# Column tile by column tile in three matmul stages, and PSUM evictions of the low-rank FFN moved from ScalarE to VectorE

## What is computed

```python
x = x + 0.5 * ffn(layernorm(x))
x = x + attn(layernorm(x))
x = x + 0.5 * ffn(layernorm(x))
def ffn(x):                       # ranks 1024 -> 256 -> 4096 -> 256 -> 1024
    P = x @ U1
    H = gelu(P @ V1 + b1)
    Q = H @ U2
    return Q @ V2 + b2
def attn(x):
    h, gate = split(x @ in_proj_w.T)          # 2048 each
    h = (causal_conv4(h, groups=8) + conv_b) * silu(gate)
    m = silu(layernorm(h) @ fc_w.T + fc_b) @ cproj_w.T + cproj_b
    return (m + h) @ out_w.T
```

## Time and profile before

| | us |
|---|---|
| median of 3 runs | 1602.27 (1602.11 to 1605.39) |
| profiled execution | 1608.78 |
| its span on the slowest core (5) | 1607.7 |
| spans of the 8 cores | 1594.6 to 1607.7 |
| TensorE matmul busy | 1158.5 (72%) |
| VectorE busy | 484.2 (30%) |
| ScalarE busy | 428.1 (27%) |
| mean granted TensorE clock, core 5 | 0.885 |

### The profile page before, as it was taken

The page is one execution under the profiler, slowest core; times in us unless marked ns, Lnnn a source line. Parts: engine busy times, 40 slices in busy tenths (PEclk is TensorE's granted clock), DMA queues, the critical chain, the costliest instruction groups (busy, mean ns, idle before and its releaser), DMA issues.

```text
span 1607.7 us, 15188 instructions; the slowest of 8 cores (1594.6 to 1607.7 us)
## 1 busy us (share of the span) xinstructions
PE 1158.5 (72%) x5480; PEld 472.9 (29%) x5480; DVE 484.2 (30%) x606; ACT 428.1 (27%) x776; POOL 23.2 (1%) x47
## 2 busy tenths in 40 slices
PE   0348744999955999847754876389997399986675
PEld 0023211444421444312322322134443044432232
DVE  0162144112247033252125222421213802324311
ACT  0344431121120100124544443212122110011444
POOL 0000000000000000000000000000000000000000
PEclk9969976999985999979986899689999599998899
DMA  9700000234220333260110000023242024420011
GB/s 144 174 1 0 1 1 0 54 65 79 43 49 1 76 60 75 53 160 27 53 53 1 1 0 0 1 40 79 40 79 53 0 53 79 79 53 0 0 53 53
DMA packets 14296, 73.65 MB, mean 46 GB/s; under 512 B 2576, under 2 KB 2576, under 8 KB 8720
## 3 DMA queue, kind: packets, MB, share of 16 engines
q0 software_dynamic: 6208, 55.58, 18.7%
q1 hardware_dynamic: 8016, 17.10, 3.1%
HBM read 119.86 MB, written 8.39 MB: 80 GB/s over the span
## 4 chain that ended last, share of the span: by engine, by line
PE 61%; DVE 17%; ACT 10%; issue 6%; DMA 4%; another core or an unknown queue 1%; DVEq 0%; ACTq 0%; POOL 0%; SPq 0%; POOLq 0%
PE pb L779 8%; PE pb L516 8%; PE pb L833 7%; PE pb L810 7%; PE pb L1022 7%; PE pb L1074 7%; PE pb L987 6%; ACT h L507 5%; PE pb L498 5%; DVE varb L396 3%; DVE hn L947 3%; DMA wslot<-ip_blob 3%; DMA y<-outb 2%; DVE xcur_sb L665 1%; DVE xn L741 1%
## 5 line engine op out<-in xcount | busy, mean ns | idle before, releaser
L507 ACT ACTIVATE h<-pb,consts_sb 128x512 bf16<-128x512 f32 (+1 forms) x320 | 165.2, 620 | 116.0 <-PE pb L498 115.8
L516 PE MATMUL pb<-h,ffn_sb 128*128 128x512 bf16 (+1 forms) x640 | 122.0, 344 | 58.3 <-ACT h L507 58.3
L987 PE MATMUL pb<-hn,wslot 128*128 128x512 bf16 x512 | 133.7, 416 | 38.6 <-DVE hn L947 37.9
L779 PE MATMUL pb<-xn,wslot 128*128 128x512 bf16 (+1 forms) x768 | 135.4, 324 | 34.5 <-DVE xn L749 34.5
L498 PE MATMUL pb<-h,ffn_sb 128*128 128x512 bf16 (+1 forms) x640 | 138.4, 350 | 20.9 <-ACT h L477 10.2
L850 DVE SCALAR_TENSOR_TENSOR h<-pb,consts_sb,gate 128x512 bf16<-128x512 f32 x64 | 48.0, 751 | 294.1 <-PE pb L833 294.0
L833 PE MATMUL pb<-ph,wslot 128*128 128x512 bf16 x512 | 116.0, 379 | 0.0
L810 PE MATMUL pb<-xn,wslot 128*128 128x512 bf16 x512 | 115.7, 379 | 0.0
L1074 PE MATMUL pb<-h,wslot 128*128 128x512 bf16 x512 | 113.3, 379 | 3.4 <-DVE h L1037 3.4
L791 ACT CAST ph<-pb 128x512 bf16<-128x512 f32 (+1 forms) x96 | 43.6, 454 | 262.6 <-PE pb L779 262.5
L1022 PE MATMUL pb<-m,wslot 128*128 128x512 bf16 x512 | 110.8, 379 | 2.6 <-ACT m L1001 2.6
(11 more groups left out here) (89 smaller groups left out, 946.1 us busy)
## 6 DMA issues: line engine op xcount, KB each, us to landing
wslot<-ip_blob POOLq DMA_DIRECT2D x16, 1536.0 KB, 12.4
wslot<-fc_blob POOLq DMA_DIRECT2D x8, 1024.0 KB, 8.1
wslot<-cp_blob POOLq DMA_DIRECT2D x8, 1024.0 KB, 8.1
wslot<-ow_blob POOLq DMA_DIRECT2D x8, 1024.0 KB, 8.2
y<-outb SPq DMA_DIRECT2D x32, 256.0 KB, 2.1
ffn_sb<-ffn_blob POOLq DMA_DIRECT2D x1, 5120.0 KB, 36.8
xcur_sb<-x SPq DMA_DIRECT2D x1, 4224.0 KB, 23.2
xcur_sb<-x SPq DMA_DIRECT2D x2, 2048.0 KB, 63.4
```

The source lines that it names most:

```text
L507: c2 = E.inc("s", s.activation(Hqb[:, mq * 512:mq * 512 + w], pt[bi][:, :w], AF.Gelu_apprx_tanh, bias=ccol("b1", m), scale=1.0))
L516: ii = t.matmul(pt[u2[mu]][:, :w], fftile("U2", k, mu), Hqb[:, kq * 512:kq * 512 + w], start=(qq == 0 and kq == 0), stop=(qq == 3 and kq = ...
L779: ii = t.matmul(pt[bi][:, :w], ws_tile(ci, "ip", ("Wh", k, ml)), xn[:, k * TH + tcol:k * TH + tcol + w], start=(k == 0), stop=(k == 7))
L987: ii = t.matmul(pt[fcb_banks[si5]][:, :w], ws_tile(ci, "fc", ("fc", m % 2, k)), hn[:, k * HT + t0o:k * HT + t0o + w], start=(k == 0), stop ...
```

## The change

- The two copies of P and the two of Q in ffn_tile go from ScalarE to VectorE (tensor_copy). There are five tiles in a half.
- In fc, cproj and out_w the column tile becomes the outer loop and k the inner one. A tile's bank is evicted behind its own matmuls, and in out_w flush3() is called between the two tiles' matmuls. In cproj the same is done as in fc.
- dst_add2: VectorE computes 0.5 * product + bias from PSUM into the outb slot (tensor_scalar) and then adds the residual to the slot in a second operation. ScalarE's multiplication and tsl are gone.

```diff
@@ -472,12 +472,12 @@
                         cnt = E.inc("t", ii)
                         E.note_w("t", bk, cnt)
                         E.note_r("t", B_xsrc, cnt)
-                        E.r_wait("s", bk)
-                        E.w_wait("s", B_Pb_c[0])
-                        c2 = E.inc("s", s.copy(Pb_c[0][:, m * 512:m * 512 + w],
-                                               pt[bi][:, :w]))
-                        E.note_r("s", bk, c2)
-                        E.note_w("s", B_Pb_c[0], c2)
+                        E.r_wait("v", bk)
+                        E.w_wait("v", B_Pb_c[0])
+                        c2 = E.inc("v", v.tensor_copy(Pb_c[0][:, m * 512:m * 512 + w],
+                                                      pt[bi][:, :w]))
+                        E.note_r("v", bk, c2)
+                        E.note_w("v", B_Pb_c[0], c2)
                     if after_u1 is not None:
                         after_u1()
                     u2a = nb(held=avoid)
@@ -523,12 +523,12 @@
                                 E.note_w("t", banks[u2[mu]], cnt)
                     for mu in range(2):
                         bk = banks[u2[mu]]
-                        E.r_wait("s", bk)
-                        E.w_wait("s", B_Qb_c[0])
-                        c2 = E.inc("s", s.copy(Qb_c[0][:, mu * 512:mu * 512 + w],
-                                               pt[u2[mu]][:, :w]))
-                        E.note_r("s", bk, c2)
-                        E.note_w("s", B_Qb_c[0], c2)
+                        E.r_wait("v", bk)
+                        E.w_wait("v", B_Qb_c[0])
+                        c2 = E.inc("v", v.tensor_copy(Qb_c[0][:, mu * 512:mu * 512 + w],
+                                                      pt[u2[mu]][:, :w]))
+                        E.note_r("v", bk, c2)
+                        E.note_w("v", B_Qb_c[0], c2)
                     for m in range(8):
                         bi = nb(held=avoid)
                         bk = banks[bi]
@@ -976,31 +976,26 @@
                                 ccol("fc_b", m, 1)))
                             E.note_r("v", bk, c2)
                             E.note_w("v", B["fcb"], c2)
-                        fcb_banks = [nb(), None]
-                        fcb_banks[1] = nb(held=(fcb_banks[0],))
-                        for bi in fcb_banks:
-                            E.w_wait("t", banks[bi])
-                        for k in range(16):
-                            E.wait("t", "vc", hn_ready[k])
-                            for si5, (tcol, w) in enumerate(OWN_TILES):
-                                t0o = tcol - HALO
-                                ii = t.matmul(pt[fcb_banks[si5]][:, :w],
+                        for (tcol, w) in OWN_TILES:
+                            t0o = tcol - HALO
+                            bi = nb()
+                            bk = banks[bi]
+                            E.w_wait("t", bk)
+                            for k in range(16):
+                                E.wait("t", "vc", hn_ready[k])
+                                ii = t.matmul(pt[bi][:, :w],
                                               ws_tile(ci, "fc", ("fc", m % 2, k)),
                                               hn[:, k * HT + t0o:k * HT + t0o + w],
                                               start=(k == 0), stop=(k == 15))
-                                if k == 15:
-                                    cnt = E.inc("t", ii)
-                                    E.note_w("t", banks[fcb_banks[si5]], cnt)
-                        E.note_r("t", B_hn, E.cnt["tc"])
-                        for si5, (tcol, w) in enumerate(OWN_TILES):
-                            t0o = tcol - HALO
-                            bk = banks[fcb_banks[si5]]
+                            cnt = E.inc("t", ii)
+                            E.note_w("t", bk, cnt)
+                            E.note_r("t", B_hn, cnt)
                             E.r_wait("s", bk)
                             E.w_wait("s", B_m1)
                             E.r_wait("s", B["fcb"])
                             c2 = E.inc("s", s.activation(
                                 m1[:, m * HT + t0o:m * HT + t0o + w],
-                                pt[fcb_banks[si5]][:, :w], AF.Silu,
+                                pt[bi][:, :w], AF.Silu,
                                 bias=fcb[:, m:m + 1], scale=1.0))
                             E.note_r("s", bk, c2)
                             E.note_w("s", B_m1, c2)
@@ -1011,31 +1006,26 @@
                         ci = half * 20 + 12 + m // 4
                         if m % 4 == 0:
                             ws_ensure(ci)
-                        cpb = [nb(), None]
-                        cpb[1] = nb(held=(cpb[0],))
-                        for bi in cpb:
-                            E.w_wait("t", banks[bi])
-                        for k in range(8):
-                            E.r_wait("t", B_m1)
-                            for si5, (tcol, w) in enumerate(OWN_TILES):
-                                t0o = tcol - HALO
-                                ii = t.matmul(pt[cpb[si5]][:, :w],
+                        for (tcol, w) in OWN_TILES:
+                            t0o = tcol - HALO
+                            bi = nb()
+                            bk = banks[bi]
+                            E.w_wait("t", bk)
+                            for k in range(8):
+                                E.r_wait("t", B_m1)
+                                ii = t.matmul(pt[bi][:, :w],
                                               ws_tile(ci, "cp", ("cp", m % 4, k)),
                                               m1[:, k * HT + t0o:k * HT + t0o + w],
                                               start=(k == 0), stop=(k == 7))
-                                if k == 7:
-                                    cnt = E.inc("t", ii)
-                                    E.note_w("t", banks[cpb[si5]], cnt)
-                        E.note_r("t", B_m1, E.cnt["tc"])
-                        for si5, (tcol, w) in enumerate(OWN_TILES):
-                            t0o = tcol - HALO
-                            bk = banks[cpb[si5]]
+                            cnt = E.inc("t", ii)
+                            E.note_w("t", bk, cnt)
+                            E.note_r("t", B_m1, cnt)
                             base = m * HT + t0o
                             E.r_wait("v", bk)
                             E.r_wait("v", B["consts"])
                             E.dep("v", B_h)
                             c2 = E.inc("v", v.scalar_tensor_tensor(
-                                h[:, base:base + w], pt[cpb[si5]][:, :w],
+                                h[:, base:base + w], pt[bi][:, :w],
                                 ccol("cproj_b", m, 1), h[:, base:base + w],
                                 ALU.add, ALU.add))
                             E.note_r("v", bk, c2)
@@ -1064,25 +1054,19 @@
                     if m % 2 == 0:
                         ws_ensure(ci)
                     for si, (tcol, w) in enumerate(OWN_TILES):
+                        t0o = tcol - HALO
                         bi = mm_banks[si][m % 2]
-                        E.w_wait("t", banks[bi])
-                    for k in range(16):
-                        E.r_wait("t", B_h)
-                        for si, (tcol, w) in enumerate(OWN_TILES):
-                            t0o = tcol - HALO
-                            bi = mm_banks[si][m % 2]
+                        bk = banks[bi]
+                        E.w_wait("t", bk)
+                        for k in range(16):
+                            E.r_wait("t", B_h)
                             ii = t.matmul(pt[bi][:, :w],
                                           ws_tile(ci, "ow", ("ow", m % 2, k)),
                                           h[:, k * HT + t0o:k * HT + t0o + w],
                                           start=(k == 0), stop=(k == 15))
-                            if k == 15:
-                                cnt = E.inc("t", ii)
-                                E.note_w("t", banks[bi], cnt)
-                    E.note_r("t", B_h, E.cnt["tc"])
-                    for si, (tcol, w) in enumerate(OWN_TILES):
-                        t0o = tcol - HALO
-                        bi = mm_banks[si][m % 2]
-                        bk = banks[bi]
+                        cnt = E.inc("t", ii)
+                        E.note_w("t", bk, cnt)
+                        E.note_r("t", B_h, cnt)
                         flush3()
                         base = m * HT + t0o
                         E.r_wait("v", bk)
@@ -1186,24 +1170,22 @@
 
                     def dst_add2(m, bi, bk, _si=si, _t0o=t0o, _tcol=tcol, _w=w):
                         sl = m % 2
-                        E.r_wait("s", bk)
-                        E.w_wait("s", B_tsl[sl])
-                        c3 = E.inc("s", s.mul(tsl[:, sl * 512:sl * 512 + _w],
-                                              pt[bi][:, :_w], 0.5))
```

(20 more changed lines are left out.)

## The result

The changed kernel took 1626.5 us (median of 8 runs), the kernel before 1605.4 on the same chip: a ratio of 1.014, 95% interval 1.0124 to 1.0156, so 21 us slower by the medians and 22 to 23 by the ratio. Forecast were +12.3 us and a range that ended at 1623. The sign was right; the size was not. (In some executions, whatever the kernel, cores of one half of the chip ran at a lower granted clock and took longer; the ratios and intervals leave these out, the medians do not.)

What follows compares the result with a forecast made beforehand. TensorE holds 61% of the chain of waits, so VectorE or ScalarE edits matter only where TensorE waits. Gains of 24.4 and losses of 36.7 make +12.3 us on 1602.3, so 1614.6 us; range 1603 to 1623.

Steps and rivals of the forecast that it cites:

- The out_w stage: In out_w, matmuls of one column tile cover the other's statistics chain: period 9.41 to 8.15 us, gain 10.5 per half.
- What VectorE pays for PSUM copies: A VectorE copy of 128x512 f32 from PSUM takes 0.69 us, 0.62 start to start; bounds 0.42 and 0.69.
- VectorE reads PSUM fast: Rival: VectorE's copies from PSUM take 0.42 us each, so the net is +1.0 us, 1603; chance 0.12.
- fc, m=0: In fc's first m, 15 matmuls formerly hidden come after hn is ready: 3.25 us lost per half, 6.5 in all.
- P copies: In FFN 1, copies queue on VectorE behind other work: per half +5.8 us in tile 2, +1.2 tile 1, +0.4 tile 0.
- The stage borders: At two stage borders one eviction remains: waits of 1.35 and 1.71 us become 0.77 and 0.85, gaining 1.44 per half.
- The output of FFN 2: Both VectorE operations hold the store slot, so output pairs come 3.85 or 3.69 us apart; loss 14.6 us together.
- the -0.25 for each tile 0: In FFN 2's tile 0 the P copy is 0.1 us slower but ScalarE's casts come sooner: -0.25 us per half.
- Tile 1 of half 1: In half 1's FFN 2, tile 1's hidden layer starts at 1558.2 against 1554.49: at most +3.7 us.
- The last tile's outputs: FFN 2's tile 1 outputs take 14.0 us against 11.0: +2.9 us in half 0, +2.3 at the kernel's end.
- the clock stays down longer: Rival: 10 more slow matmuls at each of four TensorE restarts add 8.4 us, net +20.7, 1623; chance 0.15.
- the likeliest case: The prediction's own sum of terms, net +12.3 us, with own range +7 to +18 (1609 to 1620); chance 0.68.

Runs made afterwards that it cites:

- the paired version: Loop order of fc, cproj and out_w alone, but fc's m=0 keeps both column tiles under each k; 1581.1 us, 0.985 of the kernel before.
- the best version: Loop order with fc's m=0 paired, plus four FFN 2 store slots instead of two, ScalarE still multiplying; 1565.0 us, 0.9743 of the kernel before.

## Why the prediction was right and wrong

**Right.** *The out_w stage*: period 8.16 against 8.15, gain 77.64 - 67.32 = 10.3 against 10.5. *What VectorE pays for PSUM copies*: 0.69, start to start 0.60 where I had 0.62; "VectorE reads PSUM fast" fell. *fc, m=0*: some 6 us by the paired version, 6.5 forecast, of which 5 lie in the edited stage. *P copies*: +6.3 in tile 2 against +5.8; tile 1's row product on core 3 comes 33.0 us after the reciprocal instead of 31.35, +1.65 against 1.2 + 0.4. The two FFN 1 stages together gave +15.9 against +15.2; that they agree so well is partly luck, since one by one they gave +9.7 and +6.2 for 7.6 each. *The stage borders* gave half: 1.35 became 1.21 (first row of cproj, core 3) and 1.71 became 1.07, in place of 0.77 and 0.85.

**Wrong.** The step that failed is "The output of FFN 2", whose 14.6 was mis-sized (its four terms measure 5.5 + 6.0 + 3.4 + 2.7 = 17.6), and beside it the -0.25 for each tile 0 (+0.9 and +0.7). For FFN 2 as a whole the terms make +14.5 (14.6, -0.5 and 0.4 of the Q copies); +19.3 was measured, 4.8 more. By medians over the cores, from TensorE's marks in the two stages:

- *Tile 1 of half 1*, 2.3. I priced it "from 1542.3 with 3.85" against 1554.49, "less because one store was late there already", as +3.7. That late store was the slowest core's own (its stage took 128.0 us, the median core's 125.59). From the output product of tile 0 to tile 1's hidden layer the cores lost +6.0; half 0 lost +5.5 against +5.7 forecast. That wait has two causes where I had one: the release of the banks (the output alone has +2.4 and +2.7) and the P copies behind the outputs.
- *Tile 0 of both halves*, 2.1. From the P product to the hidden layer I had -0.25 each; it was 6.11 before and 7.03 after, and 6.60 and 7.32. The copy and its hand-over are some 0.1 of that. The rest is the product itself: its 16 matmuls took 5.3 us on every core before and 5.6 or 6.5 after, in half 1 5.8 and 6.4. With no P copy moved, the output change alone shows 6.5 in half 1 on seven cores of eight, and the loop order alone 6.3 to 6.4 on six. So it is the clock's level at the restart and not the copies; that it moves with the shift in time is my reading, which no run tested by itself.
- *The last tile's outputs*, 0.9: +3.4 and +2.7 where "+2.9" and "+2.3" stood (its own figures make 3.0 and 2.2). The first operation takes 748 ns, not 690.

These are 5.3; half 0's tile 1 and the pieces between, up to 0.6 each and of both signs, give 0.5 back. Further misses: 1.0 in the normalization-to-out_w stages (mostly the borders), 0.7 in FFN 1, 0.3 in conv, 0.2 at the start. Together 7.0: +19.3 by the median core where I had +12.3. From there to the 24.2 us between 1602.3 and 1626.5, 3.1 are the baseline (three runs gave a median of 1602.3, eight 1605.4), and 1.8 are left. They are not a wider spread of the cores: in the timed runs the slowest core lies 4.6 us above the median core after the change and lay 3.9 to 6.1 above it before. They fit a profile before that was some 3 us long. So the forecast missed the median core by about 9 us, of which the stages show 7.0.

Of the rival "the clock stays down longer" a part may have come true: 192 matmuls per core at the lower level against 180, by the count described with the Q copies, 12 x 0.211 = 2.5 us where it had 8.4. But core by core the count moved by -30 to +40, so these 12 alone do not show it.

**Do the parts add up?** Not all. By the median core of the timed runs: loop order -17.0, P +22.6, output +16.2, Q +8.2, together +30.0; the whole has +21.5. The P copies are worth 22 to 23 alone and in the whole. Without them the whole has -0.6, and the other three parts add up to +7.4. The 8 us between are about what the Q copies cost alone beyond my 0.8; in the whole that cost is not there. (Sums over stages, 16.2 to 19.5 for the parts and 19.3 for the whole, seem to agree, but the output's part in them counts the cores at the lower clock.) Nor do the stages add up one by one. Half 1's fc restart costs +1.86 in the kernels with Q or output alone and nothing with P alone. Half 1's FFN 1 moves by -3.75 in the loop order with no edit of its own there; in the profile before, five cores took 148.7 to 149.4 us in it and three 144.9 to 145.5, so a part of this can be the reference's own. What I gave as the own range of the likeliest case, +7 to +18, had no allowance for such shifts of the clock, nor for a baseline of three runs; with some 3 us for each its upper end would have been about where the time fell.

## What to carry to other kernels

Moving an operation to an "idler" engine puts it behind everything that engine has queued: look first at what stands ahead of it in program order and who waits (here eight bias adds and a square; 22 to 23 us for 20 copies, four of them narrow). Where an engine writes into a store slot, count how long the slot is held and let the operation that frees a PSUM bank not wait for it; two more slots were worth 16 us. A dependent chain is best hidden behind a whole block of other matmuls, but not where the producer is the slow one: there pair up the work to use the wait.

Price a phase on the median core, not on the slowest: a late store there is luck, not slack. And hold the profiled execution against the timed ones before its stages serve as a reference: here it was 3 us long, a quarter of the forecast.

## What the runs showed of the hardware

- VectorE's plain copy of 128x512 from f32 in PSUM takes 686 and 692 ns by group, a two-scalar operation 748 (750 with the output change alone), ScalarE's cast 588.
- The same restart came out at different granted clocks in kernels that do not differ there: 0.82 and 29 matmuls, or 0.60 and 21 (restart 7.6 us later), in the 7.5 us from the restart of half 1's fc. Kernels whose only edit is the Q copies had 193 and 201 matmuls at the lower level, before 180, the loop order alone 170, the best version 164 (some 16 of each are gaps of missing records).
- After a wait of 0.82 us the hidden layer's matmuls ran at the upper level (3.85 us); after 3.82 to 7.60 us in part at the lower (5.80 to 6.54). Between these both are seen: in half 1 of the changed kernel tile 1's 16 first products took 3.61 us after 2.23 of waiting on core 3 and 5.30 after 2.51 on core 0.
